# Two accumulating transfers per scan step in a fused Mamba and FFN layer: half of each tile's state products summed by DMA

## The reference, cut to what matters

```python
def step(h, inp):                       # for each of 4096 times; h: 2048 channels x 16 states
    x_t, dt_t, B_t, C_t = inp
    dA = jnp.exp(dt_t[..., None] * A)
    dBx = dt_t[..., None] * B_t[:, None, :] * x_t[..., None]
    h = dA * h + dBx
    y = jnp.einsum('bdn,bn->bd', h, C_t)
    return (h, y)
...
y = (ys + D_param[None, :, None] * xc) * jax.nn.silu(z)
return jnp.einsum('bdl,hd->blh', y, out_proj_w)
...
x = x + _L0_attn_ref(_layernorm(x), ...)
x = x + (jnp.einsum('bsi,oi->bso', _layernorm(x), W) + bias)
```

## Time and profile before

| | |
|---|---|
| median of 3 runs | 4657.14 us (4652.04 to 4660.07) |
| the profiled execution's own time | 4652.27 us |
| its span in the profile | 4650.4 us |
| mean granted TensorE clock | 0.98 of full speed |
| busy: PE, DVE, POOL, ACT | 95%, 90%, 87%, 76% of the span |

### The profile page before, as it was taken

One profiled execution on the slowest core, in us unless ns is written; L12 is line 12 of the kernel. 1 busy time (PEld: TensorE's weight loads), 2 busy tenths in 40 slices (PEclk: granted clock), 3 DMA queues, 4 the chain that ended last, 5 costly groups with the idle time before them and its releaser, 6 DMA issues.

```text
span 4650.4 us, 80289 instructions
## 1 busy us (share of the span) xinstructions
PE 4425.4 (95%) x26656; PEld 4020.1 (86%) x26656; DVE 4164.3 (90%) x5745; ACT 3537.7 (76%) x8848; POOL 4034.5 (87%) x2942
## 2 busy tenths in 40 slices
PE   7788999999999999999999999999999999998879
PEld 6577889989898998989899898998989899897769
DVE  3899999999999999999999899999999999999871
ACT  3787787877878787787878878787887878777650
POOL 0898989989899998989899899999989999899870
PEclk9889999999999999999999999999999999999889
DMA  7324344353544435353444535335353443533232
GB/s 252 135 82 160 104 156 147 121 184 129 184 137 159 147 129 179 137 181 128 150 156 137 186 122 184 128 131 191 120 184 129 175 144 115 184 129 135 96 106 84
DMA packets 160286, 678.57 MB, mean 146 GB/s; under 512 B 21120, under 2 KB 30080, under 8 KB 110720
## 3 DMA queue, kind: packets, MB, share of 16 engines
q1 hardware_dynamic: 141440, 639.88, 39.6%
q10 hardware_dynamic: 18432, 33.56, 1.9%
HBM read 618.32 MB, written 55.05 MB: 145 GB/s over the span
## 4 chain that ended last, share of the span: by engine, by line
PE 65%; DVE 14%; POOL 8%; issue 7%; DMA 3%; ACT 2%; SPq 1%; POOLq 0%; DVEq 0%; ACTq 0%
PE gx L594 15%; PE ys L574 13%; PE g L767 12%; PE ys L614 12%; DVE hb L1378 9%; PE g L689 6%; POOL dbx L486 5%; DVE hc L1326 3%; POOL half L494 2%; PE ys L604 2%; PE ys L624 2%; PE hb L875 1%; DVE gx L1270 1%; DMA b_scratch<-ssmT 1%; DMA ybuf<-in_wf_scales 1%
## 5 line engine op out<-in xcount | busy, mean ns | idle before, releaser
L1378 DVE TENSOR_TENSOR_SCAN hb<-hb,dbx 128x512 f32<-128x512 f32 x2048 | 2496.7, 1219 | 110.8 <-ACT hb L1083 77.2
L486 POOL TENSOR_TENSOR dbx<-dtx,bb 128x1024 f32<-128x1024 f32 x1024 | 2421.2, 2364 | 68.9 <-DVE hb L1378 43.9
L1083 ACT ACTIVATE hb<-dt,a_neg 128x256 f32<-128x256 f32 x4096 | 1789.3, 468 | 66.3
L494 POOL TENSOR_TENSOR half<-hc 128x512 f32<-128x512 f32 x1024 | 1305.3, 1275 | 86.0 <-DVE hc L1326 85.1
L1326 DVE TENSOR_TENSOR hc<-hb,cb 128x512 f32<-128x512 f32 x2048 | 1376.2, 672 | 0.0
L574 PE MATMUL ys<-half,ident 128*128 128x256 f32 x4096 | 1057.2, 390 | 115.4 <-POOL half L494 99.1
L574 PEld LDWEIGHTS ys<-half,ident 128*128 128x128 f32 x4096 | 764.1, 194 | 242.9 <-POOL half L494 131.4
L767 PEld LDWEIGHTS g<-wo,ybuf 128*128 128x128 f32 x7680 | 909.3, 194 | 27.5 <-issue 15.2
L614 PE MATMUL ys<-xnT,wz 128*128 128x256 f32 x4096 | 931.5, 381 | 1.3 <-DVE ybuf L1337 1.3
L594 PE MATMUL gx<-xnT,wx 128*128 128x256 f32 x3968 | 903.6, 382 | 21.8 <-issue 11.0
L767 PE MATMUL g<-wo,ybuf 128*128 128x128 f32 x7680 | 915.0, 277 | 9.0 <-issue 9.0
(11 more groups left out here) (105 smaller groups left out, 2739.1 us busy)
## 6 DMA issues: line engine op xcount, KB each, us to landing
wz<-in_win SPq DMA_DIRECT2D x128, 1024.0 KB, 4.8
wx<-in_win SPq DMA_DIRECT2D x124, 1024.0 KB, 4.8
wo<-in_wout SPq DMA_DIRECT2D x123, 1024.0 KB, 5.0
wf<-wf_scratch SPq DMA_DIRECT2D x113, 512.0 KB, 3.9
xc_scratch<-xcn ACTq DMA_DIRECT2D x128, 256.0 KB, 3.7
xcs<-xc_scratch SPq DMA_DIRECT2D x128, 256.0 KB, 5.0
bb<-bc_scratch SPq DMA_DIRECT2D x64, 512.0 KB, 8.8
cb<-bc_scratch SPq DMA_DIRECT2D x64, 512.0 KB, 8.0
```

Source lines behind the costliest of these rows:

```text
L486: nc.gpsimd.tensor_tensor(dbx[:, k % 2, :].rearrange("p (n t) -> p n t", n=NQ), dtx[:, S % 2, a, :].unsqueeze(1).to_broadcast([P, NQ, T]), ...
L494: nc.gpsimd.tensor_tensor(half[:, k % 4, :], hc[:, k % 2, 0:HALF], hc[:, k % 2, HALF:GW], ALU.add).then_inc(halves, 1)
L1083: ins = nc.scalar.activation(h[:, m * T:(m + 1) * T], dt[:, j % 2, a, :], ACT.Exp, scale=a_neg[:, ds((2 * j + a) * N + 2 * v + m, 1)])
L1378: nc.vector.tensor_tensor_scan(h[:], h[:], dbx[:, k % 2, w * UW:(w + 1) * UW], 0.0, ALU.mult, ALU.add).then_inc(scans, 1)
```

## The change

GpSimd no longer sums the first two groups (q = 0 and 1) of a tile one by one. VectorE writes their products into a new buffer `hd`, and GpSimd issues a transfer that adds the second group's 128 x 1024 products onto the first's within SBUF (`add_group_pair`). One sum (`pair_sum`) then stands for both groups. Groups 2 and 3 keep `hc` and their own sums. A step has 6 sums in place of 8, and TensorE adds 6 in place of 8. The bias is added by one accumulating transfer per chunk in place of four GpSimd additions. The orders of GpSimd and TensorE are rewritten, and `y_gate(S, 0)` moves behind scan 11 and product 10.

```diff
+        hd = sb("hd", [P, 2, GW])
...
-            def group_sum(S, k):
-                pool.wait_ge(hcs, after(UNITS * S + 2 * k + 2))
-                pool.wait_ge(sum_mm, after(8 * S + k - 3))
-                nc.gpsimd.tensor_tensor(half[:, k % 4, :], hc[:, k % 2, 0:HALF], hc[:, k % 2, HALF:GW],
+            def add_group_pair(S, a):
+                pool.wait_ge(hcs, after(UNITS * S + UNITS // 2 * a + 4))
+                pool.dma_start(hd[:, 0, :], hd[:, 1, :], accum_op=ALU.add).then_inc(hd_acc, 16)
+            def pair_sum(S, a):
+                pool.wait_ge(hd_acc, 16 * (2 * S + a + 1))
+                nc.gpsimd.tensor_tensor(sum_place(S, FIRST_TWO[a]), hd[:, 0, 0:HALF], hd[:, 0, HALF:GW],
                                         ALU.add).then_inc(halves, 1)
+            def group_sum(S, a, q):
+                pool.wait_ge(hcs, after(UNITS * S + UNITS // 2 * a + 2 * q + 2))
+                i = 3 * a + (2 if q == NQ - 1 else a)
+                nc.gpsimd.tensor_tensor(sum_place(S, i), hc[:, q % 2, 0:HALF], hc[:, q % 2, HALF:GW],
+                                        ALU.add).then_inc(halves, 1)
...
-                for i in range(4):
-                    add_bias(chunk, i)
+                pool.dma_start(x2_rows(chunk % 2), ffn_bias.partition_broadcast(P).unsqueeze(1).to_broadcast([P, TT, H]),
+                               accum_op=ALU.add).then_inc(bias_add, 16)
...
-                    for k in range(1, 8):
-                        if k == 7 and zz:
-                            inflow_of(S + 1)
-                        group_of_b(S, k, c)
-                        if k >= 2:
-                            group_sum(S, k - 2)
...
+                    products(1)
+                    if not (first and c == 0):
+                        group_sum(S - 1, 1, 3)
+                    products(2)
+                    add_group_pair(S, 0)
+                    products(3)
+                    products(4)
+                    group_sum(S, 0, 2)
+                    pair_sum(S, 0)
+                    products(5)
+                    group_sum(S, 0, 3)
+                    if first and st.ffn:
+                        add_bias(c - 2)
+                    products(6)
+                    add_group_pair(S, 1)
+                    if zz:
+                        inflow_of(S + 1)
+                    products(7)
+                    pair_sum(S, 1)
                     if zz:
                         carry_of(S + 1)
                         group_of_b(S + 1, 0, (S + 1) // PAIRS)
-                    group_sum(S, 6)
+                    group_sum(S, 1, 2)
...
-                nc.vector.tensor_tensor(hc[:, k % 2, w * UW:(w + 1) * UW], hb[u % 4][:],
-                                        cb[:, n:n + 2, :].rearrange("p n t -> p (n t)"), ALU.mult
+                dst = (hd if q < 2 else hc)[:, q % 2, w * UW:(w + 1) * UW]
+                nc.vector.tensor_tensor(dst, hb[u % 4][:], cb[:, n:n + 2, :].rearrange("p n t -> p (n t)"), ALU.mult
...
                     z_in_proj(1)
-                    group(4)
+                    group(3)
                     z_in_proj(0)
-                    group(5)
```

More of the change, by code:

```diff
@@ L28 @@
 UNITS = 4 * NQ
+SUMS = 6
+FIRST_TWO = (1, 3)
+HS = 4
 UW = 2 * T
@@ L538, in step, with products @@
                     zz = st.next_scan(last)
-                    for k in range(1, 8):
-                        if k == 7 and zz:
-                            inflow_of(S + 1)
+                    def products(k):
                         group_of_b(S, k, c)
-                        if k >= 2:
-                            group_sum(S, k - 2)
-                        elif not (first and c == 0):
-                            group_sum(S - 1, 7)
-                        if k == 5 and j % 2 == 0 and st.ffn:
-                            add_bias(c - 2, j // 2)
+                    products(1)
[17 more added lines that the diff above has]
+                    pair_sum(S, 1)
                     if zz:
@@ L560, in _, with group_sum @@
             iterations(iteration)
-            group_sum(NC * PAIRS - 1, 7)
+            group_sum(NC * PAIRS - 1, 1, 3)
             for chunk in (NC - 2, NC - 1):
-                for i in range(4):
-                    add_bias(chunk, i)
+                add_bias(chunk)
         @block.tensor
         def _(pe):
-            def group_sum(SG, k):
-                a, q = divmod(k, NQ)
-                pe.wait_ge(halves, after(8 * SG + k + 1))
-                for i in range(2):
-                    mm = nc.tensor.matmul(ys[a][:, 0:T], ident[:], half[:, k % 4, i * T:(i + 1) * T],
-                                          start=False, stop=(q == NQ - 1 and i == 1), skip_group_check=True)
+            def group_sum(SG, i):
+                pe.wait_ge(halves, after(SUMS * SG + i + 1))
+                for w in range(2):
+                    mm = nc.tensor.matmul(ys[i // 3][:, 0:T], ident[:], half[:, (SUMS * SG + i) % HS, w * T:(w + 1) * T],
+                                          start=False, stop=(i % 3 == 2 and w == 1), skip_group_check=True)
                 mm.then_inc(sum_mm, 1)
@@ L812, in step @@
                         x_proj()
-                        group(0)
                         out_proj(2)
@@ L1332, in y_gate @@
                 chunk, jp = divmod(SP, PAIRS)
[L1333 removed]
+                dve.wait_ge(sum_mm, after(SUMS * SP + 3 * (a + 1)))
                 dve.wait_ge(sz_act, after(SP + 1))
@@ L1465, in step @@
                     product(9)
+                    scan(11)
+                    product(10)
                     if not (last and st.norm1):
                         y_gate(S, 0)
-                    scan(11)
-                    product(10)
                     scan(12)
@@ L1493, in last_ffn @@
             def last_ffn(chunk, j):
-                dve.wait_ge(bias_add, after(4 * chunk + j // 2 + 1))
+                dve.wait_ge(bias_add, 16 * (chunk + 1))
                 dve.wait_ge(f_mm, after(chunk * PAIRS + j + 1))
@@ L1498, in _ @@
             times_c(LAST - 1, UNITS - 1)
-            dve.wait_ge(bias_add, after(4 * (NC - 2)))
+            dve.wait_ge(bias_add, 16 * (NC - 2))
             dve.wait_ge(f_mm, after(LAST - 2 * PAIRS))
```

64 lines of the change are left out of this document (30 added, 34 removed).

## The result

| | before | after |
|---|---|---|
| median | 4655.44 us (4 runs, 4652.04 to 4660.07) | 5663.51 us (4 runs, 5628.86 to 5678.12) |
| ratio, 95% interval | | 1.2154 [1.2092, 1.2215] |
| span in the profile | 4650.4 us | 5673.2 us |
| mean granted TensorE clock | 0.98 | 0.918 |

The change costs a fifth of the time. 5290 was forecast, with a range of 4830 to 5750, which holds the result; but the result lies in the rival "long transfers" (over 5450, chance 0.14), not in the forecast's own case (5050 to 5450, chance 0.54).

A forecast was written before the change was run, and what follows sets the result against it. TensorE bounded ordinary steps (33.20 us); after the change, a loop between VectorE's FFN additions: 34.76 plus issues and landing gives 37.87, plus 1.68 clock gives 39.55. With the edges, 630 us on 4652 gave 5290, range 4830 to 5750.

The forecast's parts named there:

- long transfers: Rival: a landing of 7.0 us at both transfers delays the pair's sums; loop 42.6 us, time about 5660, chance 0.14.
- 1 to 3: VectorE's FFN addition to product 11, 20.35 us, plus GpSimd stalls at the first transfer and the work queued behind it.
- X: Time that issuing one transfer holds GpSimd, taken as 1.0 us within bounds of 0.33 and 1.27; twice in the loop.
- 4 and 5: GpSimd's second issue after product 11, then the larger of 3.69 us of queued work and the landing, 4.8.
- 6, 7 and the clock: GpSimd's pair sum 1.27 us, TensorE's sum, z part and FFN block 8.26, plus 1.68 for lowered clock.
- Step 2: First transfer waits for product 3 and holds up `dbx` of group 3, stalling VectorE's scan 6 by about 1.6 us.
- Step 3: GpSimd's work behind the first transfer, 9.76 us against the 9.23 VectorE allows, stalls scan 10 by 0.53.
- Step 5: Second transfer's landing, taken as 4.8 us, outlasts the 3.69 of `inflow_of` and `dbx` of 7; pair sum waits about 1.1.
- Clock: TensorE's gap ahead of its sum between the z parts lowers its clock; z part 5.30 instead of 3.62, adding 1.68 us.
- First steps: First step of a chunk, with the bias's issue ahead of `dbx` of 6: 40.35 us against 39.3 before.
- Cheap rival: Issue 0.33 us, landing at most 3.69, no clock loss; loop 35.42 us, time 4810; chance 0.20 for 4750 to 5050.
- Faster rival: TensorE's relief reaches the step, GpSimd's waits fall in slack, VectorE's 32.2 us bounds; 4515 us, chance 0.08.

The follow-up runs named there:

- The filled gap: The changed kernel with 24 unread identity products (5.4 us) on TensorE between the z part and the wait for the pair sum; 5658.19 us.
- the first experiment: The changed kernel, with SyncE starting the 1 MB load of `wo` only when the step's second accumulating transfer has landed; 5186.67 us.
- the last experiments: Five versions of the changed kernel with the whole computation kept and GpSimd's and TensorE's work reordered to hide the transfers; 4829.54, 4718.04, 4719.27, 4680.28 and 4674.01 us.
- the fourth: The reordered kernel with sums first (4718.04 us), with TensorE's order changed in the first and last step of a chunk alone; 4680.28 us, ratio 1.007 to before.
- the run with issues alone: The changed kernel with each step's two transfers replaced by unread 64 KB ones, the second group's products left out of the sum; 5088.54 us.

## Why the prediction was right, and where its sizes were off

The direction, the loop and the range held; the median came out 374 over the forecast. That it stayed in the range is in part luck. The prediction gave a landing over 6.2 as a sign of being wrong, and the second one took 8.0 in its terms; the forecast's 4.8 lies between the two values that the runs show (3.7 and 8.0) and is neither. The 5660 of the rival "long transfers" came within 4 us, but from a landing of 7.0 at both transfers, where the first landed in 3.7 and the second in 8.0. In the step of 44.04 (1521.97 to 1566.01), by the prediction's terms:

| term | forecast | measured |
|---|---|---|
| 1 to 3, with the first X and the hop: addition to second issue | 22.54 | 22.96 |
| 4 and 5: second issue to the pair's sum (X + L) | 5.8 | 9.00 |
| 6, 7 and the clock: pair's sum to addition | 11.21 | 12.08 |
| loop | 39.55 | 44.04 |

- **Step 2, 0.56 + X.** Right: 1.64 idle ahead of scan 6, forecast 1.6. X is 0.92 up to the end of the next instruction.
- **Step 3, 0.53.** Right: 0.59 ahead of scan 10, and the first pair's sum waits for nothing.
- **Step 5, L = 4.8.** This is the mis-sized term. Alone the transfer lands 4.6 behind the start of its issue, 3.7 behind X, so it would be just hidden (3.69 of other work). Beside the load of `wo` it takes 8.9, so L is 8.0. The 3.2 that the prediction set beside it, with a time of about 5150, was 3.7 in the run with the later load (5187 us), and the first byte of about 1 that it quoted is a first packet 1.44 behind the issue. The prediction had checked the mean load of the DMA engines and what a transfer takes, not which transfer starts in the same tenth of a microsecond. The load, in another queue and issued later, makes the transfer 4.3 longer and becomes 1.2 longer itself (6.2 against 5.0). The Trainium skill (DMA: Bandwidth & Descriptors, section Queues, rings and completion order) says that a DMA engine takes turns between the queues that have work, a packet at a time. The trace shows no such turns between these two: from 1546 to 1550 it has 134 packets of the load's queue and none of the transfer's. Whether one of the turns that the Trainium skill names can be as long as a whole load, no run shows.
- **Clock, 1.68.** Its size was off, and its source did not carry over. In the run with the later load the gap is 2.56, about that of the earlier trace rows, and the sum and the z part run at full rate: with the landing just hidden the term is nothing, and a gap about 1.1 longer, as at the forecast's landing, is in no run. The loss comes with the gap of 6.87 that the collision makes. TensorE's granted clock is 0.50, the lower of its two levels, from 1553.5 to 1560.2; from the pair's sum to the FFN block it is 8.23, and 5.80 in the run with the later load, so 2.43. The filled gap shows that it is real in the long steps; its worth in the total isn't measured, since the filler took as much elsewhere.
- **Short steps.** Not foreseen: 14 of the 78 ordinary steps of chunks 2 to 14 take 37.7 to 38.9. In the one read above the low clock delays the load.
- **First steps, 40.35.** Under-sized, 45.8. I took the bias's landing to have a whole step of time. It has, but the second tile's transfer stands behind it in GpSimd's queue, and SyncE loads 1 MB of `x` rows 1.8 behind the bias. In the run with the later load, where `wo` is out of the way, the second transfer needs 9.5 in a first step and 4.6 in others:

```profile
1668.83 1.19 POOL L526 DMA_DIRECT2D x<-in_ffn_bias  x1
1670.59 0.38 SPq L383 DMA_DIRECT2D xrow<-in_x  x1
...
1674.56 0.90 POOL L507 DMA_DIRECT2D hd<-hd  x1 [2.15 <-DVE hd L1357]
...
1684.08 1.26 POOL L512 TENSOR_TENSOR half<-hd 128x512 f32<-128x512 f32 x1 [4.84 <-DMA hd<-hd]
```

  The bias alone is not the cause. The first step of chunk 14 issues it at the same place but has no rows left to load, and there the same transfer lands in 4.57 and its sum doesn't wait:

```profile
4453.73 1.18 POOL L526 DMA_DIRECT2D x<-in_ffn_bias  x1
...
4459.45 0.90 POOL L507 DMA_DIRECT2D hd<-hd  x1 [2.15 <-DVE hd L1357]
...
4464.08 1.26 POOL L512 TENSOR_TENSOR half<-hd 128x512 f32<-128x512 f32 x1
```

  The bias lands in 7.7 there, and in 9.3 to 11.5 in the twelve first steps with rows, where the second transfer takes 8.4 to 10.6. The 64 KB transfers show the same, 5.6 to 7.2 against 2.8. So it is a second collision, of the bias with the load of rows. A run with the bias elsewhere was not made, so whether the load of rows would be enough without it stays open.
- **The sum.** Over the chunk from 1428.57 to 1770.38 it is 341.81, forecast 317.2. 24.6 more in each of 14 chunks would be 344 of the 391 by which the span lies over 5282. Over the whole kernel, the way from the first FFN block to the last is 939 longer than before where 584 were forecast, which is 355, and the first block comes 83 later where 46 were forecast, which is 37: chunk 1 has the collision too, in five of its eight steps.
- **Bias.** Right: worth nothing by itself, though beside its transfer the load of `x` rows lands in 9.5 in place of 4.9 (medians); nobody waits for that there.
- **Cheap rival.** Its landing was right for a transfer alone, 3.7. With no collision the time is 5187 by the first experiment and not 4810, since the issue is 0.92 by its row, 1.12 in the loop, and not 0.33, and the first steps stay long.
- **Faster rival.** It needed terms 4 to 7 and the stalls 1.6 + 2X shorter. The orders of the last experiments do that: in the fourth, 78 ordinary steps win 36 us, but 13 first steps lose 54 and 13 last ones 6.

## What to carry to other kernels

Look at what other transfers start within a microsecond of a new one that somebody waits for, and behind which event they are released; a mean DMA share says nothing about that. What counts is whose packets begin first, not who is issued first: here SyncE's load was issued behind GpSimd's transfer and still went ahead. And when an order is changed, read this phase again, since the change itself moves it. When a sum is handed to a transfer, cost the issue on the issuing engine (about 1 us here, against the 1.23 us of the sum it saves) and everything queued behind the wait for its data. A transfer pays only where its issue fits into the engine's idle time and its landing has other work in front of it: place both ends before judging the idea.

## What the runs showed of the hardware

- A 512 KB accumulating transfer within SBUF, issued by GpSimd, landed in 4.6 alone, in 8.7 to 9.5 with a 1 MB load issued 0.09 to 0.26 behind it on SyncE, in 5.0 to 5.8 with that load 1.73 to 1.76 behind it. One of 64 KB landed in 2.4 alone and in 5.6 to 6.5 with the load 0.1 to 0.2 behind it.
- In the collision read above the load's packets came first, nearly all of them, and the transfer's from 5.13 behind its issue. Where nothing was ahead of it, the transfer had its first packet 1.44 behind its issue on GpSimd; the load had its first 0.95 to 0.99 behind its issue on SyncE.
- With a 1 MB accumulating transfer 5.7 ahead in its own queue the transfer landed in 4.57; with a 1 MB load 4.0 ahead as well, in 8.4 to 10.6.
- An issue of 64 KB was recorded as long as one of 512 KB on GpSimd (median 0.89 both, 0.86 to 1.04).
- The length of TensorE's gap doesn't decide alone whether the clock falls: behind 2.56 and 1.57 nothing was slower, behind 6.87 the sum took 2.04 instead of 1.10 at a granted clock of 0.50, and in the run with issues alone the output projection took 5.27 instead of 3.73 behind a gap of 1.53, where the same gap left it at 3.73 without transfers.
